# The four products of a long job in one run behind the state product, in eleven of sixteen slots of the delta stage

## The reference, cut to what matters

```
q, k, v = causal_conv_silu(x @ W)          # 16 heads of 128; a convolution over 4 steps
g    = -exp(A_log) * softplus(x @ Wfa @ Wfb + dt_bias)
beta = sigmoid(x @ Wb)
# per head, over the sequence, with S of 128 x 128:
S  = S * exp(g_t)[:, None]
vd = (v_t - S^T k_t) * beta_t
S  = S + k_t vd^T
o_t = S^T q_t
out = (o * rsqrt(mean(o^2)) * o_norm_w * sigmoid(x @ Wga @ Wgb)) @ Wo
```

## Time and profile before

| | |
|---|---|
| median of three runs | 3431.48 us |
| the profiled execution: its own time / its span | 3426.05 / 3424.3 us |
| delta stage with units 0 to 15 on PE (L1566 first to last) | 928 to 2782 us |
| one unit (unit 5, slots 0 to 15) | 1521.7 to 1638.5 us |
| PE busy / ACT busy / DVE busy, share of the span | 95% / 43% / 63% |

### The profile page before, as it was taken

One profiled execution on the slowest core, in us unless ns is written; L12 is line 12 of the kernel. 1 busy time (PEld: TensorE's weight loads), 2 busy tenths in 40 slices (PEclk: granted clock), 3 DMA queues, 4 the chain that ended last, 5 costly groups with the idle time before them and its releaser, 6 DMA issues. The chain is left out here.

```text
span 3424.3 us, 78381 instructions
## 1 busy us (share of the span) xinstructions
PE 3244.6 (95%) x33424; PEld 1534.5 (45%) x33424; DVE 2156.9 (63%) x3546; ACT 1480.1 (43%) x3401; POOL 125.6 (4%) x457
## 2 busy tenths in 40 slices
PE   7989999996889999999999999999999868999999
PEld 4444444443444444444444444444444434444443
DVE  2354524415788888889878988878898625451441
ACT  2031101104456756766675676567667533110110
POOL 0000000000000000000000000000000000000000
PEclk9999999998989999999999999999999878999999
DMA  3022222114101111121121211101211012222121
GB/s 120 0 64 69 74 86 68 55 49 165 34 27 33 57 52 40 39 70 43 31 67 40 63 40 48 42 28 55 67 42 33 18 68 89 74 75 85 62 55 62
DMA packets 99289, 195.72 MB, mean 57 GB/s; under 512 B 10248, under 2 KB 35464, under 8 KB 96384
## 3 DMA queue, kind: packets, MB, share of 16 engines
q1 hardware_dynamic: 98944, 190.71, 17.5%
HBM read 173.64 MB, written 17.04 MB: 56 GB/s over the span
## 5 line engine op out<-in xcount | busy, mean ns | idle before, releaser
L1624 PE MATMUL psum<-dl_xt,dl_wqkv 128*128 128x512 f32 x1536 | 762.6, 620 | 9.7 <-DVE dl_qkv L1268 9.6
L1268 DVE SCALAR_TENSOR_TENSOR dl_qkv<-psum,dl_par,dl_qkv 128x511 f32<-128x511 f32 (+2 forms) x576 | 428.7, 744 | 32.5 <-ACT dl_tails L1107 23.5
L481 PE MATMUL psum<-xnt_sb,wmats 128*128 128x512 f32 x896 | 408.3, 593 | 2.2 <-DVE f_partial L707 2.2
L1624 PEld LDWEIGHTS psum<-dl_xt,dl_wqkv 128*128 128x128 f32 x1536 | 262.6, 190 | 265.0 <-issue 229.0
L481 PE MATMUL psum<-f_token_sums,wmats 128*128 128x512 f32 x672 | 306.8, 592 | 0.0
L707 DVE TENSOR_TENSOR f_partial<-f_partial,psum 128x512 f32<-128x512 f32 x112 | 76.9, 687 | 310.2 <-PE psum L481 308.8
L481 PEld LDWEIGHTS psum<-xnt_sb,wmats 128*128 128x128 f32 x896 | 169.4, 190 | 218.0 <-issue 212.0
L596 ACT ACTIVATE f_partial<-psum 128x512 f32<-128x512 f32 x32 | 19.1, 597 | 550.6 <-PE psum L481 550.6
L1631 PE MATMUL psum<-dl_wo,dl_sg 128*128 128x512 f32 x512 | 256.7, 620 | 0.3 <-DVE dl_sg L1471 0.3
L1103 ACT ACTIVATE dl_qkv<-psum,dl_par 128x512 f32<-128x512 f32 x192 | 148.9, 776 | 194.5 <-PE psum L1624 194.5
L537 PE MATMUL psum<-f_wdown,f_hidden_a 128*128 128x512 f32 x512 | 224.3, 592 | 0.0
(11 more groups left out here) (217 smaller groups left out, 4713.2 us busy)
## 6 DMA issues: line engine op xcount, KB each, us to landing
dl_wqkv<-in_dw_qkv SPq DMA_DIRECT2D x192, 256.0 KB, 2.6
f_wdown<-in_wdowns SPq DMA_DIRECT2D x64, 512.0 KB, 3.5
wmats<-in_wmats SPq DMA_DIRECT2D x56, 512.0 KB, 3.5
dl_wo<-in_dwo SPq DMA_DIRECT2D x16, 1024.0 KB, 5.2
f_weights_b<-f_weights_by_expert SPq DMA_DIRECT2D x24, 512.0 KB, 9.5
x_sb<-in_x SPq DMA_DIRECT2D x4, 1024.0 KB, 9.1
x_after_experts<-x_sb SPq DMA_DIRECT2D x16, 256.0 KB, 2.6
xn_transposed<-xnt_sb SPq DMA_DIRECT2D x4, 1024.0 KB, 5.9
```

What stands on the lines that cost most here:

```text
L481: ins = pe.matmul(ps[:, bank, :], wm[:, m % WRING, block, k, :], moving[:, k, :], start=(fresh and k == 0), stop=(last_of and k == 1), ski ...
L1268: tap_ = lambda dl: dve.scalar_tensor_tensor(y_[:, dl:TT], ps[:, bank, 0:TT - dl], par[:, h, 4 * a + 3 - dl:4 * a + 4 - dl], y_[:, dl:TT], ...
L1624: last = pe.matmul(ps[:, bank, :], wq[:, n % RING, m, :], xt[:, u // HG % 2, m, :], start=(m == 0), stop=(m == KC - 1))
```

## The change

In slots 0 to 5 and 11 to 15 the four products of the long job are issued in one run behind the state product. The short jobs of these slots are spread anew: one in front of the u product (place "long") and one behind it (place "inner"), and what stood at "end" for gates and decays moves forward. The second halves of `cross` and `corner` and the job `beta` stay at "end". Slots 6 to 10 keep their order. ACT's copies of the short jobs follow the new places (so gate and decay copies come ahead of the tap); DVE's order is the same as before. In slot 12 and 13 `dec` now stands before `krow`.

```
-             (4, "inner"): [("turn", p, 0, every), ("turn", p, 1, every)],
+             (4, "long"): [("turn", p, 0, every)], (4, "inner"): [("turn", p, 1, every)],
...
-             (12, "inner"): [("krow", w, 0, every), ("dec", w2, 2, every)],
+             (12, "long"): [("dec", w2, 2, every)], (12, "inner"): [("krow", w, 0, every)],
...
+                        halves = 6 <= sl <= 10
-                        if job:
+                        if job and halves:
                             long_job(job, (0, 1))
                         all_short(k, sl, "long")
                         if run:
                             solve_u(k, sl)
                         all_short(k, sl, "inner")
-                        if job and not filler:
+                        if job and halves and not filler:
                             long_job(job, (2,))
                         if run:
                             state_step(k, sl)
-                        if job and filler:
+                        if job and not halves:
+                            long_job(job, (0, 1, 2))
+                        elif job and filler:
                             long_job(job, (2,))
                         all_short(k, sl, "split")
                         if job:
```

More of the change, by code:

```diff
@@ L818, in short_jobs @@
     every, first, second = None, (0, 1), (2, 3)
[L819 to L822, removed]
-             (4, "inner"): [("turn", p, 0, every), ("turn", p, 1, every)],
-             (5, "inner"): [("turn", p, 2, every), ("turn", p, 3, every)],
+    table = {(0, "long"): [("krow", k, 3, every)], (0, "inner"): [("vrow", k, 1, every)],
+             (1, "long"): [("vrow", k, 2, every)], (1, "inner"): [("vrow", k, 3, every)],
+             (2, "long"): [("gate", p, 0, every)], (2, "inner"): [("gate", p, 1, every)],
+             (3, "long"): [("gate", p, 2, every)], (3, "inner"): [("gate", p, 3, every)],
+             (4, "long"): [("turn", p, 0, every)], (4, "inner"): [("turn", p, 1, every)],
+             (5, "long"): [("turn", p, 2, every)], (5, "inner"): [("turn", p, 3, every)],
              (6, "states"): [("level", w, 0, first)], (6, "inner"): [("level", w, 0, second)],
@@ L827, in short_jobs @@
              (8, "end"): [("sums", w, 0, every)],
-             (11, "inner"): [("dec", w2, 0, every)], (11, "end"): [("dec", w2, 1, every)],
-             (12, "inner"): [("krow", w, 0, every), ("dec", w2, 2, every)],
-             (13, "inner"): [("krow", w, 1, every), ("dec", w2, 3, every)],
-             (14, "inner"): [("cross", w, 0, first), ("krow", w, 2, every)], (14, "end"): [("cross", w, 0, second)],
-             (15, "inner"): [("vrow", w, 0, every), ("corner", w, 0, first)], (15, "end"): [("corner", w, 0, second)]}
+             (11, "long"): [("dec", w2, 0, every)], (11, "inner"): [("dec", w2, 1, every)],
+             (12, "long"): [("dec", w2, 2, every)], (12, "inner"): [("krow", w, 0, every)],
+             (13, "long"): [("dec", w2, 3, every)], (13, "inner"): [("krow", w, 1, every)],
+             (14, "long"): [("cross", w, 0, first)], (14, "inner"): [("krow", w, 2, every)], (14, "end"): [("cross", w, 0, second)],
+             (15, "long"): [("vrow", w, 0, every)], (15, "inner"): [("corner", w, 0, first)], (15, "end"): [("corner", w, 0, second)]}
     once = {(4, "end"): ("beta", w, 0, every), (7, "end"): ("ga", w, 0, every), (9, "end"): ("fa", w2, 0, every)}.get((sl, at))
```

## The result

The changed kernel takes **3502.31 us** (median of 4 runs, 3496.44 to 3507.56) against 3429.99 us for the kernel before on the same chip: ratio **1.0213 [1.0193, 1.0233]**, 72 us slower. The forecast was 3487. The profiled executions differ by 76.2 us: spans of 3500.5 and 3424.3 us.

A forecast was written before the change was run, and what follows sets the result against it. PE was taken to set the pace, busy 115.08 of 116.8 us a unit. Slot terms of 33.6 and 25.1 us, together 58.7, on the profiled 3426.05 gave 3484.8; half of 5.4 on top made 3487 us, range 3445 to 3532.

The forecast's parts named there:

- Direction and mechanism: Without half a long job before u, PE's state product waits for ACT's copy of u; the kernel gets 58.7 us slower.
- the u product of slot 12: Slot 12: u stays at 3.62 us, held by DVE; PE stands 1.74 us instead of 0.78, slot +0.86.
- the second turn of slot 5: Slot 5: this turn waits for the bank DVE's L1471 reads and starts at 3.20 us; slot +1.01.
- The terms of the slots: Growth per slot: 2.24 us in slots 0 to 6 (15 units), 1.79 in slots 12 to 15 (14 units).
- the date T+3.17: Earliest state product after slot start T: ACT's other work over at T+2.77, plus 0.40 us from copy start.
- Slot 15's term: Slot 15: the vrow before u waits for DVE's L1432 and starts 0.32 us late, less 0.19: +0.13.
- its own rival: PE's breaks drop the clock to half speed: one fall a unit 3509 us, two 3532; chance 22%.
- Slots 2, 3 and 11 cost nothing: In these slots 512-column jobs around u bring PE to the state product at 3.18 us, late as ACT: 0.
- the points that would have made it wrong: State product before T+3.0 in slots 1 and 4, unit under 118 us, or clock below 0.97 in units 1 to 13.
- The rival by which ACT's hand-over is not the bound: ACT takes u as soon as it is there; only exits and old waits count: faster, 3392 us; chance 5%.
- the one by which only the slots that wait for DVE cost in full: Only slots 5, 12 and 0 cost in full, about half the loss: 1.6 us a unit, 3449 us; chance 11%.
- the one by which DVE sets the unit: DVE, busy 85%, and not PE sets the length of a unit, so nothing changes; chance 4%.

The follow-up runs named there:

- the run with the filled break: The changed kernel with the dec product in front of u in slot 12 done twice (same result): 3497.67 us, ratio 1.0201 to the kernel before.
- the last experiment: The kernel before with three of the four long products in front of u in slots 5, 6 and 12: 3431.39 us, ratio 1.0007.

## Why the prediction was right, and where it was not

**Direction and mechanism: right.** *The state product now can't start before ACT is done with tap, decay, output and squares.* The slots of the changed kernel show it (no bracket on L1090), and the run without squares shows it by moving both by the half microsecond that was left out. The other two waits named ahead, the u product of slot 12 and the second turn of slot 5, stand in the list of waits with 1.57 and up to 2.0 us.

**The terms of the slots: right within 0.12 us each.** The common error is the date T+3.17. The copy does not wait for the end of L1085's read of the accumulator: it starts at T+2.68, 0.08 before that row ends, and the state product is at T+3.07 or 3.08 in slots 1, 4, 13 and 14. That takes 0.1 us from each of these terms. Slot 15's term was 0.11 too large (+0.02). By the measured terms the sum would be 50.6 instead of 58.7 us.

**The clock: its own rival was right in part, and this is the step that failed in the forecast's sum.** The sum had no fall; the rival had one or two in every unit. There are 9 more than before in units 0 to 13: 5 behind slot 12's break, 3 in slot 5 of units with a beta job, and 1 in slot 2 of unit 0. At 1.6 to 1.7 us each, near the size that the prediction took from the earlier trace rows, that is about 15 us. The traces of all kernels here together show that longer breaks go with them (the counts stand in the last section); the run with the filled break fits this. The Trainium skill (TensorE: Matmul & The Clock Gate, section "Why this matters for your kernels") warns of longer gaps only; breaks of 1.57 us here had a fall behind them in 5 of 12 slots 12, so the trace goes against it as a safe bound.

**Units with a beta job (3, 7, 11): not seen.** The job stands in the rotation of the two banks, so in slot 5 it is now the *first* turn that must wait for L1471, in front of u. Slot 5 of unit 3 in the changed kernel begins at 1339.20:

```profile
1342.23 0.74 DVE L1471 SCALAR_TENSOR_TENSOR dl_sg<-psum,dl_onw,dl_sg 128x512 f32<-128x512 f32 x1
...
1343.03 0.66 PE L1709 MATMUL psum<-constants_sb,dl_val 128*128 128x128 f32 x4 [2.02 <-DVE dl_sg L1471]
1343.61 0.42 PE L1593 MATMUL psum<-dl_rbuf,dl_zd 32*32 32x128 f32 x8
...
1345.36 4.91 PE L1631 MATMUL psum<-dl_wo,dl_sg 128*128 128x512 f32 x8
1350.20 0.42 PE L1566 MATMUL psum<-dl_state,dl_kq 128*32 128x128 f32 x8
```

The state product comes behind u, so the whole chain moves: the slot is 11.0 us, 9.4 without its clock fall, where it was 7.37 before. That is 1.0 us beyond the ordinary slot 5's cost, three times. The prediction read an ordinary unit alone.

**The account.** 50.6 us of slot terms, 15 of clock falls, 3 of beta units: 69. In units 1 to 13 alone, 45 of terms, 12 of falls and 3 of beta units make 60 of the measured 61.2. Unit 0 has no short jobs in slot 2, and that slot takes 8.83 us instead of 5.74:

```profile
951.22 0.50 PE L1604 MATMUL psum<-dl_ubuf,dl_kkt 32*128 32x128 f32 x8 [1.75 <-ACT dl_ubuf L1090]
951.65 5.40 PE L1624 MATMUL psum<-dl_xt,dl_wqkv 128*128 128x512 f32 x8
```

It is the same wait for ACT, with nothing on PE to cover it, and half speed behind it. The start of unit 0 is 5.8 us later in the profiled run (934.0 instead of 928.2), and how much of this is the change's is open. In all six kernels with the new order in slots 13 to 15, PE waits 4.4 to 5.6 us for DVE's blocks (L1426) ahead of unit 0, and the unit starts at 933.0 to 934.4; in the seven with the old order that wait is 0.9 to 2.6 us, but the start varies from 928.2 to 934.4. Of the 76.2 us, 2 are left. The forecast had 58.7 us for all this: its slot terms were 8 too large, and the falls, the beta units and the start were missing, so the errors partly cancel, by luck, and 3487 is only 15 us below the median.

**"Slots 2, 3 and 11 cost nothing": right in sum, wrong as a property of these slots.** Alone, slot 2 costs 0.72 us; it is free only behind a stretched slot 1. In the same way slot 1 costs 0.77 us instead of 0.15 when slot 0 keeps its old order. The terms are right as a set and don't add up singly: the three groups of slots, changed alone, cost 84 us together, all at once 72.

**What was to show it:** L1604's wait for L1090 is 40.0 us in the list, but the over 30 us of new idle time that was named for slots 1, 4, 13 and 14 is not there: 16.3 of the 40.0 stood before the change, and these slots have 22.4. The unit lasts 120.4 us (121), PE's share falls from 95% to 93% with nearly the same busy time (3244.6 and 3252.1 us), and the granted clock of units 1 to 13 is 0.99. None of the points that would have made it wrong occurred. The rival by which ACT's hand-over is not the bound is out by the state product at T+3.08; the one by which only the slots that wait for DVE cost in full is out, since slots 1, 4, 13 and 14 cost 1.3 us a unit together; the one by which DVE sets the unit is out by the unit's 3.6 us.

## What to carry to other kernels

Long products between two steps of a chain between engines are the cover for the other engine's work: before taking them away, date that engine's copy, counted from the event that its whole list hangs on, and set it against PE's new date for the product. Where the other engine is late, do the opposite and move a product in front of the waiting one (slot 12: -0.3%), but look at what stands behind the moved hand-over on that engine, since slot 6 took it all back. Before turning an engine's list round, ask what has a date behind the item moved: work that lay in a wait costs nothing where it is, and cost 1% where it was put here.

## What the hardware showed that I had not expected

- **Half speed behind short breaks.** Of 12 breaks of 1.54 to 1.57 us in slot 12 of the changed kernel, alike in length and surroundings, 5 were followed by a half-speed stretch, which makes the run of eight 5.40 instead of 3.70 us. The 13 traces here have these breaks of PE from 0.6 us up in units 1 to 13: of 203 up to 1.3 us none was followed by half speed, of 46 from 1.4 to 1.6 us 9 were, and of 48 from 1.7 us up 36. The same break can go either way: 1.56 us in slot 12 had none in the run with ACT's list turned round. What decides within a length is open, and so is how much the small products on both sides of a break matter, since no run changed them alone.
- **An activation does not wait for the read of the accumulator before it.** The row of L1085's read is 1584.16 to 1584.34 and the copy L1090 starts at 1584.26, 0.08 us before that row ends. Rows of other neighbouring activations overlap in the same way: the tap's ends at 1582.47, and the decay's starts at 1582.42.
- **A table load of 1.28 us and nothing on top.** In the rows of the last experiment the copy ends at 1562.99, the load stands from 1563.01 to 1564.29, and the silu starts at 1564.30. The Trainium skill (ScalarE: Activation LUTs, section "What ACT_TABLE_LOAD costs") gives the same 1283 ns for the load; the drain of about 1380 ns that it adds for every switch does not appear between these rows, so here the measurement decides for 1.28.
